# One-core decoder layer on Trainium2: spectral weights folded first and piece by piece, value projection moved into attention step 0, three later weights split during mixing steps 0 and 1

## The chip, the cores and the metric

The kernel runs on one core of a Trainium2 chip. The metric is the device time of one execution in microseconds (us). The engines are named as in the profile: PE is TensorE (its weight loads are PEld), DVE is VectorE, ACT is ScalarE, POOL is GpSimd, and SP is SyncE, which issues all DMAs of this kernel.

## The reference, cut to what matters

Eight sequences of 512 tokens of width 512 go through three sublayers, each with a residual and a layer norm:

```python
qkv = x @ w_qkv                        # 512 x 1536, then an FFT over each head of 64
kv = cumsum(fft(k) * fft(v), axis=1)   # along the tokens
x = layernorm(x + ifft(kv * conj(fft(q))).real @ w_out)

q, k, v = x @ W_q + b_q, ctx @ W_k + b_k, ctx @ W_v + b_v    # ctx: 8 x 77 rows, 16 heads of 32
x = layernorm(x + softmax(mask(q @ k.T / sqrt(32))) @ v @ W_o + b_o)

w = clip(round(kernel / s), -8, 7) * s           # s = max|kernel| / 7
x = layernorm(x + x @ w + bias + (x @ a) @ b)
```

## The kernel before, in words

The program has three stages, each a block with its own instruction list for every engine. The order in every list is written by hand; semaphores tie the lists together.

**Preparation (`prepare`).** It turns inputs and weights into what the loops need. Every operand of a big product is held as a high part of reduced precision (fp32r, written by ACT) and a low remainder (a subtraction by DVE or POOL), and each product is three matmuls: high by high, low by high, high by low (`split_matmuls`, line 74). In order: the 616 context rows are transposed and split; keys are projected (8 products of 12 matmuls of 308 columns) and stored to `k_dram`; values are projected (5 products of 12 matmuls of 512 columns) and stored to `v_dram`; then `w_qkv` is folded with the forward transform in 12 pieces (`turn`, then 4 products with `fwd`, which the profile counts as 8 matmuls of 128 columns) into `w_spec`; DVE quantizes the feed-forward weight in three passes of 128 x 2048 and adds the low-rank product `a @ b` (4 matmuls, `AT_LOW`); `w_out` is folded with the inverse transform (4 pieces, `AT_BACK`) into `w_back`. `raw_v` and `w_qkv` share the tile `wqkv_sb`, so most of `w_qkv` is loaded only after the split of `W_v`.

**Mixing (`mix_tokens`).** One step for each sequence. A step of PE is twelve spectral projections of 12 matmuls of 512 columns (v, v, k, k, q, q, twice), the four transposes (`turn`) of the next sequence's `x` between the first of them, and the four back projections of the sequence before. All four transposes use one PSUM bank, `xT_ps`: `turn(c)` waits until ACT and DVE have split piece c-1 (`split_x`, counted by `x_hi` and `x_lo`). Sequence 0 is transposed and split at the head of this stage. After step 0 ACT and POOL split `W_q`.

**Attention (`attend`).** Step i scores sequence i, and finishes sequence i-1. Step 0 has no earlier sequence: PE scores, transposes the probabilities, transposes `x1` of sequence 1 and projects its queries. Four PSUM banks are handed round in the order `START_ORDER`. `W_o` and the feed-forward weight are loaded raw at the head of the stage and split at the end of step 0 (by ACT and DVE, and by ACT and POOL).

Of the kernel before, what the change touches and what calls it, by code (L numbers as in the profile page):

```python
# [6 lines left out]
F32 = mybir.dt.float32  # L19
# [6 lines left out]
P = 128  # L26
# [51 lines left out]
def prepare(nc, ins, constants, half_power, ident, w_spec, w_back, k_dram, v_dram, ffn_dram, x_first, x_loaded, ffn,  # L78
            out_slots, w_k, w_v):


# [6 lines left out]
    with ExitStack() as ctx:  # L88
# [4 lines left out]
        fwd = sb("fwd_sb", [P, P])  # L93
        wT = sb("wT_sb", [P, 2, NC, P])


        ctx_tail = ffn[:, 0, :]
        inv = wqkv_sb[:, 0, 0:512].rearrange("p (h n) -> p h n", h=2)
        b_sb = wqkv_sb[0:RANK, 0, D:2 * D]

        raw_k = wout_sb[:]
        raw_v = wqkv_sb[:].rearrange("p c n -> p (c n)")[:, NC * D:2 * NC * D].rearrange("p (c n) -> p c n", c=NC)
        ctxT = [sb(f"ctxT_{k}", [P, NC, rows], F32R) for k in ("hi", "lo")]
        a_sb = ffn[:, 1, 0:NC * RANK].rearrange("p (c n) -> p c n", c=NC)
        aT = sb("aT", [RANK, D])
        bias_k = sb("bias_k", [P, NC])
        k_val = wT[:].rearrange("p a c n -> p (a c n)")[:, 0:2 * half_rows].rearrange("p (a n) -> p a n", a=2)

        out_hi, out_lo = out_slots
        SLOTS = NC  # L110
        top, top_all = sb("top", [P, 1]), sb("top_all", [P, 1])
        scale, per_scale = sb("q_scale", [P, 1]), sb("q_per_scale", [P, 1])
        turned = [ps(f"turned{n}", [P, NC * P]) for n in range(2)]
        prod = [ps(f"prod{n}", [P, D]) for n in range(2)]
        ident_loaded, constants_loaded = sem("ident_loaded"), sem("constants_loaded")
        ctx_loaded, wk_loaded, wv_loaded = sem("ctx_loaded"), sem("wk_loaded"), sem("wv_loaded")
        kernel_loaded, a_loaded, b_loaded = sem("kernel_loaded"), sem("a_loaded"), sem("b_loaded")
        fwd_loaded, qkv_loaded, out_loaded = sem("fwd_loaded"), [sem(f"qkv_loaded{r}") for r in range(NC)], sem("out_loaded")
        ctx_turned, tail_turned, ctx_hi, ctx_lo = sem("ctx_turned"), sem("tail_turned"), sem("ctx_hi"), sem("ctx_lo")
        a_turned, aT_ready, w_turned, wT_ready = sem("a_turned"), sem("aT_ready"), sem("w_turned"), sem("wT_ready")  # L120
        wk_hi_ready, wk_lo_ready, wv_hi_ready, wv_lo_ready = sem("wk_hi_ready"), sem("wk_lo_ready"), sem("wv_hi_ready"), sem("wv_lo_ready")
        prod_ready, prod_used = sem("prod_ready"), sem("prod_used")
        k_biased, k_hi_ready, k_lo_ready = sem("k_biased"), sem("k_hi_ready"), sem("k_lo_ready")
        v_hi_ready, fold_hi_ready = sem("v_hi_ready"), sem("fold_hi_ready")
        stored = [sem(f"kv_stored{n}") for n in range(SLOTS)]
# [6 lines left out]
        NKEY, NVAL = 2 * NC, len(tiles)  # L132
        GROUP = [(r, s) for r in range(NC) for s in range(3)]
        AT_V = NKEY
        AT_FOLD = AT_V + NVAL
        AT_LOW = AT_FOLD + len(GROUP)
        AT_BACK = AT_LOW + NC

        def fold_target(n):

            if n < len(GROUP):
                r, s = GROUP[n]
                return [w[:, r, s, :] for w in w_spec]
            return [w[:, n - len(GROUP), :] for w in w_back]

        def fold_place(n):
            return AT_FOLD + n if n < len(GROUP) else AT_BACK + n - len(GROUP)

        @block.sync
        def _(sp):  # L150
            flat = ins["ctx"].rearrange("b k d -> (b k) d")
            sp.dma_start(ident[:], ins["identity"]).then_inc(ident_loaded, 16)
            sp.dma_start(x_first[:], flat[0:tail, :].rearrange("(n p) d -> p n d", p=P)).then_inc(ctx_loaded, 16)
# [8 lines left out]
            for n in range(NKEY):  # L162
# [11 lines left out]
                elif 1 <= n < NC:  # L174

                    sp.wait_ge(wv_lo_ready, NC)
                    sp.dma_start(wqkv_sb[:, n, :], ins["w_qkv"][n * P:(n + 1) * P, :]).then_inc(qkv_loaded[n], 16)
# [1816 lines left out]
```

## Time and profile before

| | us |
|---|---|
| median of 3 runs | 968.82 |
| lowest and highest run | 965.21, 971.74 |
| span of the profiled execution, first to last instruction | 964.6 |
| PE busy in that span | 917.6 |
| DVE, ACT, POOL busy | 666.7, 376.8, 337.8 |

The times are of the whole execution; the span leaves out what lies before the first and behind the last instruction. The profiled execution has no time of its own in the list; its span is 0.6 us under the lowest run and 4.2 us under the median. Busy time of PE counts matmuls from their start to a modelled end, so a busy PE can still run at half clock.

### The profile page before, as it was taken

The page shows a single profiled execution, that of the slowest core. Times are in us where ns is not written, and L with a number is a line of the kernel's source. Part 1 is how long each engine was busy: PE and PEld are TensorE (multiplying, and loading weights), DVE is VectorE, ACT ScalarE, POOL GpSimd, SP SyncE. Part 2 cuts the span into 40 slices and gives each one's busy share as a digit, 9 for nine tenths or more (in the row PEclk, how much of TensorE's full clock was granted, in tenths as well). Part 3 has the DMA queues.
Part 4 walks back from the last instruction along what each step waited for, and adds up shares of the span by engine and source line. Part 5 has one row for each costly group of instructions (what it writes and reads, how often), then busy time and mean ns, then how long its engine had stood idle before and what let it go on. Part 6 is the DMA issues. An engine that isn't in the chain of part 4 may idle for free.

```text
span 964.6 us, 14638 instructions
## 1 busy us (share of the span) xinstructions
PE 917.6 (95%) x4476; PEld 754.5 (78%) x4476; DVE 666.7 (69%) x1128; ACT 376.8 (39%) x1403; POOL 337.8 (35%) x310
## 2 busy tenths in 40 slices
PE   5898999999999999999779999999999999999987
PEld 4784888888888888888668788888888888888775
DVE  3363466665656565555667888979889798887957
ACT  3152120101010111102287566656567565666610
POOL 2000243232222232324236434444443444433733
PEclk9998999999999999999979999999999999999999
DMA  5944201221203020203423122131222203120021
GB/s 179 326 148 172 90 1 52 80 80 52 104 28 127 3 87 1 88 23 116 134 81 102 25 79 73 40 113 24 89 63 78 75 21 122 30 89 21 17 77 44
DMA packets 72346, 76.02 MB, mean 79 GB/s; under 512 B 38567, under 2 KB 40871, under 8 KB 72303
## 3 DMA queue, kind: packets, MB, share of 16 engines
q1 hardware_dynamic: 72303, 75.49, 24.4%
q8 instruction: 22, 0.36, 0.2%
q14 instruction: 21, 0.17, 0.1%
HBM read 52.60 MB, written 22.87 MB: 78 GB/s over the span
## 4 chain that ended last, share of the span: by engine, by line
PE 41%; DVE 4%; ACT 2%; issue 2%; POOL 2%; POOLq 0%; DVEq 0%
PE shared_ps L74 31%; PE score_ps L74 4%; PE shared_ps L1146 4%; ACT probs L1352 2%; PE shared_ps L1109 1%; PE shared_ps L1179 1%; POOL probs L1501 1%; DVE score_ps L1658 1%; DVE xT_lo L1615 0%; DVE x_and_res L1704 0%; DVE top_s L1663 0%; DVE pT_lo L1642 0%; POOL x_and_res L1516 0%; DVE y L1682 0%; DVE w_o_lo L1825 0%
## 5 line engine op out<-in xcount | busy, mean ns | idle before, releaser
L1352 ACT ACTIVATE probs<-score_ps,top_s 128x77 f32<-128x77 f32 x512 | 159.0, 359 | 36.9 <-DVE top_s L1663 36.9
L1352 ACT ACTIVATION_READ_ACCUMULATOR probs<-score_ps,top_s 128x1 f32 x512 | 122.9, 240 | 0.0
L1501 POOL TENSOR_TENSOR probs<-probs,per_total 128x616 f32<-128x616 f32 x64 | 82.7, 1309 | 65.9 <-DVE per_total L1670 65.7
L1494 POOL TENSOR_TENSOR rstd<-ve,half_power 128x1 f32<-128x1 f32 x64 | 42.4, 662 | 157.1 <-DVE ve L1693 152.5
L722 POOL TENSOR_TENSOR vals<-qs_prod 128x512 f32<-128x512 f32 x32 | 41.1, 1296 | 127.1 <-DVE qs_prod L804 127.1
L713 POOL TENSOR_TENSOR mix_rstd<-mix_ve,half_power 128x1 f32<-128x1 f32 x32 | 22.0, 688 | 175.4 <-DVE mix_ve L823 175.4
L1658 DVE COPY_PREDICATED score_ps<-hidden,masked 128x616 f32<-128x616 int32 x64 | 66.2, 1034 | 11.6 <-PE score_ps L74 11.6
L1359 ACT ACTIVATE pT_hi<-shared_ps 103x512 fp32r<-103x512 f32 (+1 forms) x96 | 54.7, 612 | 46.0 <-PE shared_ps L1146 45.5
L672 ACT ACTIVATE v_sb<-v_ps 128x512 f32<-128x512 f32 x32 | 18.9, 594 | 133.9 <-PE v_ps L74 133.9
L679 ACT ACTIVATE qT_hi<-vals 128x512 fp32r<-128x512 f32 x32 | 19.4, 631 | 122.3 <-POOL vals L722 106.2
L1642 DVE TENSOR_TENSOR pT_lo<-shared_ps,pT_hi 103x512 fp32r<-103x512 f32 (+1 forms) x96 | 64.5, 684 | 0.0
L1146 PE MATMUL shared_ps<-ident,probs 128*103 128x128 f32 (+1 forms) x384 | 53.9, 279 | 2.6 <-POOL probs L1501 1.8
L74 PE MATMUL shared_ps<-w_o_hi,xT_hi 128*128 128x512 f32 x128 | 53.3, 417 | 2.3 <-DVE xT_lo L1623 1.9
L74 PE MATMUL shared_ps<-w_ffn_hi,xT_hi 128*128 128x512 f32 x120 | 50.1, 418 | 5.5 <-DVE xT_lo L1615 4.9
L1516 POOL TENSOR_TENSOR x_and_res<-x_and_res,bias_f 128x512 f32<-128x512 f32 x32 | 42.2, 1318 | 35.9 <-DVE x_and_res L1704 23.1
L1146 PEld LDWEIGHTS shared_ps<-ident,probs 128*103 128x103 f32 (+1 forms) x384 | 47.0, 158 | 9.7 <-POOL probs L1501 2.7
L1663 DVE TENSOR_REDUCE top_s<-score_ps 128x8 f32<-128x616 f32 x64 | 51.2, 800 | 3.6
L815 DVE TENSOR_TENSOR mix_r<-out_ps,x_res 128x512 f32<-128x512 f32 x29 | 20.1, 692 | 47.3 <-PE out_ps L74 47.3
L74 PE MATMUL v_ps<-xT_hi,w_spec_hi 128*128 128x512 f32 x128 | 50.6, 395 | 1.9 <-DVE xT_lo L766 1.9
L74 PE MATMUL k_ps<-xT_hi,w_spec_hi 128*128 128x512 f32 x128 | 51.7, 404 | 0.0
L74 PE MATMUL q_ps<-xT_hi,w_spec_hi 128*128 128x512 f32 x128 | 51.2, 400 | 0.0
L74 PE MATMUL shared_ps<-w_o_hi,xT_lo 128*128 128x512 f32 x128 | 50.7, 396 | 0.0
(218 smaller groups left out, 2660.1 us busy)
## 6 DMA issues: line engine op xcount, KB each, us to landing
x_tok<-in_x SPq DMA_DIRECT2D x8, 1024.0 KB, 5.9
x_res<-in_x SPq DMA_DIRECT2D x8, 1024.0 KB, 8.0
x_between<-mix_x SPq DMA_DIRECT2D x32, 256.0 KB, 2.0
x<-x_between SPq DMA_DIRECT2D x8, 1024.0 KB, 5.5
x_tok<-x_between SPq DMA_DIRECT2D x8, 1024.0 KB, 5.7
out<-y_out SPq DMA_DIRECT2D x32, 256.0 KB, 2.0
wqkv_sb<-in_w_qkv SPq DMA_DIRECT2D x4, 768.0 KB, 7.8
keys_split<-w_q_hi SPq DMA_DIRECT2D x8, 154.0 KB, 5.4
```

The costliest lines, as they stand in the source:

```text
L74: last = nc.tensor.matmul(out, l, r, start=(n == 0), stop=(n == len(terms) - 1))
L713: nc.gpsimd.tensor_tensor(rstd[:, t % 2:t % 2 + 1], ve[:, t % 2:t % 2 + 1], half_power[:], ALU.pow).then_inc(rstd_ready, 1)
L722: nc.gpsimd.tensor_tensor(vals[:, h, :], qs[:, 2 * h, :], qs[:, 2 * h + 1, :], ALU.subtract if h else ALU.add).then_inc(vals_summed, 1)
L1146: last = nc.tensor.transpose(shared_ps[s.bank(use)][0:size, g * P:(g + 1) * P], probs[:, t % 2, g * GK + at:g * GK + at + size], ident[:])
L1352: nc.scalar.activation(probs[:, t % 2, j * KEYS:(j + 1) * KEYS], score_ps[:, g, k * KEYS:(k + 1) * KEYS], ACT.Exp, bias=top[:, t % 2, j:j ...
L1359: nc.scalar.activation(pT[0][0:size, c, :, t * P:(t + 1) * P], turned_bank(s, t, c), ACT.Copy).then_inc(turned_hi, 1)
L1494: nc.gpsimd.tensor_tensor(rstd[:, n:n + 1], ve[:, n:n + 1], half_power[:], ALU.pow).then_inc(rstd_ready, 1)
L1501: nc.gpsimd.tensor_tensor(p, p, per_total[:, t % 2, h * heads:(h + 1) * heads].unsqueeze(2) .to_broadcast([P, heads, KEYS]), ALU.mult).the ...
L1516: nc.gpsimd.tensor_tensor(res2[:, t % 2, :], x2[:, t % 2, :], bias_f[:], ALU.add).then_inc(res2_ready, 1)
L1642: nc.vector.tensor_tensor(pT[1][0:size, c, :, tok], turned_bank(s, t, c), pT[0][0:size, c, :, tok].bitcast(F32), ALU.subtract).then_inc(fr ...
L1658: nc.vector.copy_predicated(s4, hidden[:, t, :].unsqueeze(1).unsqueeze(1).to_broadcast(shape), masked[:].unsqueeze(1).unsqueeze(1).to_broa ...
L1663: nc.vector.tensor_reduce(top[:, t % 2, h * 8:(h + 1) * 8].rearrange("p (g j) -> p g j", j=GH), s4, AX.X, ALU.max, negate=True).then_inc(t ...
```

## The change

- **Preparation** loads `w_qkv` first, in 12 pieces of 256 KB with a semaphore each, and folds them as they land. From the seventh piece on the transposes of the context ride along in four new PSUM banks (`side`, `turn_side`). Then come sequence 0 of `x`, the key projection, the low-rank product and `w_back`. The value projection is gone; the turned context is stored to a new DRAM tensor `c_dram` instead. Sequence 0 of `x` leaves this stage transposed and split. The quantization moves from DVE to POOL.
- **Mixing** starts with the projections at once. In steps 0 and 1 ACT and POOL also split `W_v`, `W_o` and the feed-forward weight, a quarter at a time through two pairs of slots, and SP stores both parts to `w_later` in DRAM. Each of the three is loaded into `x1_next` once the one before is done.
- **Attention** step 0 gets the value projection (`project_v`, 5 products of 12 matmuls, with `split_v` on ACT and DVE); split weights and turned context come from DRAM.

The core of the diff:

```diff
@@ prepare, sync @@
+            load_qkv(0, 0)
+            sp.dma_start(fwd[:], ins["dft_forward"]).then_inc(fwd_loaded, 16)
+            load_qkv(0, 1)
+            load_qkv(0, 2)
...
+            for r in (2, 3):
+                for s in range(3):
+                    load_qkv(r, s)
+            sp.dma_start(raw_k[:], by_chunk(ins["W_k"])).then_inc(wk_loaded, 16)
...
+                if n < len(tiles):
+                    at, size = tiles[n]
+                    for part, tile in enumerate(ctxT):
+                        sp.dma_start(c_dram[n, part, :, :, 0:size], tile[:, :, at:at + size].bitcast(F32)).then_inc(ctx_stored, 16)
@@ prepare, gpsimd @@
+            nc.gpsimd.tensor_scalar(ffn, ffn, per_scale[:], ROUND_MAGIC, ALU.mult, ALU.add).then_inc(quantized, 1)
...
+            nc.gpsimd.tensor_scalar(ffn, ffn, ROUND_MAGIC, -QMAX - 1, ALU.subtract, ALU.max).then_inc(quantized, 1)
...
+            nc.gpsimd.tensor_scalar(ffn, ffn, QMAX, scale[:], ALU.min, ALU.mult).then_inc(quantized, 1)
@@ mix_tokens, sync @@
-            load_x(2, 0, True)
+            load_x(2, 0, False)
+            load_residual(0)
+            for w, raw in enumerate(raw_later):
+
+                if w == 0:
+                    sp.wait_ge(wq_lo, NC)
+                else:
+                    sp.wait_ge(later_lo, w * NC)
+                sp.dma_start(x1_next[:], raw.rearrange("(c p) n -> p c n", p=P)).then_inc(later_loaded, 16)
+                for c in range(NC):
+                    n = w * NC + c
+                    sp.wait_ge(later_hi, n + 1)
+                    sp.wait_ge(later_lo, n + 1)
+                    for part in range(2):
+                        sp.dma_start(w_later[w, part, c * P:(c + 1) * P, :],
+                                     slots[n % 2][part].bitcast(F32)).then_inc(later_stored[n % 2], 16)
@@ mix_tokens, scalar @@
+            def split_later(w):
+
+                act.wait_ge(later_loaded, 16 * (w + 1))
+                for c in range(NC):
+                    n = w * NC + c
+                    wait_reuse(act, later_stored[n % 2], 32 * (n // 2))
+                    nc.scalar.activation(slots[n % 2][0], x1_next[:, c, :], ACT.Copy).then_inc(later_hi, 1)
...
+            split_later(0)
+            copy_v(0, 1, 0)
+            copy_v(0, 1, 1)
+            split_vals(0, 0, 0)
+            split_vals(0, 0, 1)
+            split_later(1)
+            split_vals(0, 1, 0)
+            split_vals(0, 1, 1)
+
+            copy_v(1, 0, 0)
+            copy_v(1, 0, 1)
+            split_later(2)
+            for c in range(NC):
+                split_x(2, 0, c)
@@ attend, sync @@
+            sp.dma_start(w_v[0].bitcast(F32), by_chunk(w_later[0, 0])).then_inc(w_v_loaded, 16)
+            load_context(0)
+            sp.dma_start(w_v[1].bitcast(F32), by_chunk(w_later[0, 1])).then_inc(w_v_loaded, 16)
@@ attend, tensor @@
             score(0, s, 1, 0)
+            project_v(s, 0)
             score(0, s, 1, 1)
+            project_v(s, 1)
             score(0, s, 2, 0)
             turn_probs(0, s, 0, 0)
             turn_probs(0, s, 0, 1)
             turn_probs(0, s, 0, 2)
+            project_v(s, 2)
...
+            project_v(s, 3)
             turn_probs(0, s, 1, 2)
             score(0, s, 3, 1)
             project_q(1, s, 0)
+            project_v(s, 4)
@@ attend, scalar @@
-            act.wait_ge(w_loaded[0], 16)
-            nc.scalar.activation(w_o[0][:], raw_o, ACT.Copy).then_inc(w_hi, 1)
...
-            act.wait_ge(w_loaded[1], 16)
-            nc.scalar.activation(w_ffn[0][:], raw_ffn, ACT.Copy).then_inc(w_hi, 1)
```

On POOL, `split_later(w)` (the remainders, counted by `later_lo`) stands in step 0 behind the `W_q` remainders for w = 0, behind the first two `remainder` calls for w = 1, and at the head of step 1 for w = 2.

## Rows read from the trace of the kernel before

**Rows 1.** The page: busy tenths of PE in 40 slices of 24.1 us.

```profile
PE   5898999999999999999779999999999999999987
```

**Rows 2.** Stretches by stage: preparation, mixing step 1, attention start.

```profile
0.00:88.00 88.00, 70.31 (x364) 55.01 (x364) 37.27 (x60) 31.81 (x59) 5.68 (x10) 0.94 0.58 192
...
125.70:165.00 39.30, 39.30 (x178) 31.59 (x178) 21.66 (x36) 8.69 (x13) 16.40 (x15) 1.00 0.05 19
...
475.00:500.00 25.00, 16.46 (x70) 15.05 (x71) 14.66 (x23) 17.84 (x102) 8.25 (x6) 0.66 0.46 146
```

The columns are start and end, length, busy time (with instructions) of PE, PEld, DVE, ACT and POOL, granted clock, DMA share, GB/s.

**Rows 3.** Timeline of PE: preparation and first mixing product (start, length).

```profile
17.20 0.59 PE L74 MATMUL prod<-ctxT_hi,xT_hi 128*128 128x308 f32 x1 [2.42 <-DVE xT_lo L352]
...
21.70 0.31 PE L74 MATMUL prod<-ctxT_lo,xT_hi 128*128 128x308 f32 x1
...
32.95 0.39 PE L74 MATMUL prod<-xT_hi,ctxT_hi 128*128 128x512 f32 x1
...
53.80 0.60 PE L251 MATMUL turned<-ident,wqkv_sb 128*128 128x128 f32 x4
54.24 1.06 PE L266 MATMUL prod<-fwd_sb,wT_sb 128*128 128x128 f32 x8
55.13 0.60 PE L251 MATMUL turned<-ident,wqkv_sb 128*128 128x128 f32 x4
...
71.26 4.03 PE L275 MATMUL prod<-wqkv_sb,aT 16*128 16x512 f32 x6 [0.36 <-DVE w_spec_lo L393]
75.22 9.36 PE L282 MATMUL prod<-wout_sb,wqkv_sb 128*128 128x512 f32 x16
...
90.09 0.51 PE L74 MATMUL v_ps<-xT_hi,w_spec_hi 128*128 128x512 f32 x1 [1.90 <-DVE xT_lo L766]
```

**Rows 4.** Two stretches of the first loads, with columns as in Rows 2.

```profile
3.00:4.00 1.00, 0.00 (x0) 0.00 (x0) 0.00 (x0) 0.00 (x0) 0.00 (x0) 1.00 0.77 219
4.00:5.00 1.00, 0.00 (x0) 0.00 (x0) 0.00 (x0) 0.00 (x0) 0.00 (x0) 1.00 1.07 387
```

**Rows 5.** Timeline of DVE in the preparation.

```profile
50.11 2.28 DVE L382 TENSOR_REDUCE top<-x 128x1 f32<-128x2048 f32 x1
...
71.12 0.68 DVE L411 TENSOR_TENSOR x<-prod,x 128x512 f32<-128x512 f32 x1
```

**Rows 6.** Groups of POOL by line: busy us, mean ns of one.

```profile
L335 POOL TENSOR_TENSOR xT_lo<-wqkv_sb,xT_hi 128x512 fp32r<-128x512 f32 x4 | 5.0, 1279 | 17.6 <-ACT xT_hi L299 17.6
...
L758 POOL MEMSET xT_hi<- 128x1232 f32 x1 | 1.1, 1130 | 0.0
```

**Rows 7.** DMA issues with us to landing: mixing start, one store, attention start.

```profile
x_tok<-in_x SPq DMA_DIRECT2D x1, 1024.0 KB, 5.1
...
x<-in_W_q SPq DMA_DIRECT2D x1, 1024.0 KB, 8.0
...
x_between<-mix_x SPq DMA_DIRECT2D x1, 256.0 KB, 2.0
...
x_tok<-in_W_o SPq DMA_DIRECT2D x1, 1024.0 KB, 6.7
```

**Rows 8.** Timeline of SP: the first DMAs of mixing and of attention.

```profile
86.22 0.38 SPq L515 DMA_DIRECT2D x_tok<-in_x  x1
...
475.46 0.39 SPq L1033 DMA_DIRECT2D x<-x_between  x1
```

**Rows 9.** Timeline of PE: two transposes in mixing step 1.

```profile
131.13 0.60 PE L565 MATMUL xT_ps<-ident,x_tok 128*128 128x128 f32 x4
134.43 0.66 PE L565 MATMUL xT_ps<-ident,x_tok 128*128 128x128 f32 x4
```

**Rows 10.** Timeline of PE in attention step 0, and the start of step 1.

```profile
484.29 0.62 PE L74 MATMUL score_ps<-xT_hi,qT_hi 128*128 128x308 f32 x1 [1.08 <-ACT probs L1352]
...
503.42 0.40 PE L74 MATMUL shared_ps<-xT_hi,w_q_hi 128*128 128x512 f32 x1
...
517.91 0.30 PE L74 MATMUL score_ps<-xT_hi,qT_hi 128*128 128x308 f32 x1
```

More of the change, by code:

```diff
@@ new lines, in _ @@
+            pe.wait_ge(ident_loaded, 16)
+            turn(0)
+            pe.wait_ge(fwd_loaded, 16)
+            for m in range(NFOLD):
+                if m + 1 < NFOLD:
+                    turn(m + 1)
+                if m == FIRST_SIDE:
+                    pe.wait_ge(ctx_loaded, 32)
+                if m >= FIRST_SIDE:
+                    turn_side(m - FIRST_SIDE)
+                pe.wait_ge(wT_ready, m + 1)
+                wait_reuse(pe, prod_used, m - 1)
+                for c in range(NC):
+                    p, h = c // 2, c % 2
+                    out = prod[m % 2][:, p * 256:(p + 1) * 256].rearrange("q (i h k) -> q i h k", i=2, h=2)[:, :, h, :]
+                    last = nc.tensor.matmul(out, wT[:, m % 2, c, :], fwd[:].rearrange("q (i k) -> q i k", i=2),
+                                            start=True, stop=True)
+                last.then_inc(prod_ready, 1)
@@ L620, in step @@
                     project(i, half, s, 1, h)
-            for c in range(NC):
-                turn(0, 0, c, first_banks[c])
             step(0, 0, True, False)
+            step(1, 1, True, True)
             steps(pe, step)
@@ L691, in step @@
                         split_vals(i, p, h)
+            copy_v(0, 0, 0)
+            copy_v(0, 0, 1)
+            split_x(1, 1, 0)
+            act.wait_ge(wq_loaded, 16)
             for c in range(NC):
[L694 to L697 removed]
+                nc.scalar.activation(w_q[0][:, c, :], x1_next[:, c, :], ACT.Copy).then_inc(wq_hi, 1)
+            split_x(1, 1, 1)
+            split_x(1, 1, 2)
+            split_x(1, 1, 3)
+            split_later(0)
[9 more added lines that the diff above has]
+            split_later(2)
+            for c in range(NC):
+                split_x(2, 0, c)
+            copy_v(1, 1, 0)
+            copy_v(1, 1, 1)
+            for p in range(PAIRS):
+                for h in range(2):
+                    split_vals(1, p, h)
             steps(act, step)
@@ L861, in step @@
                 times_q(i, 1, 1)
-            for c in range(NC):
-                split_x(0, 0, c, first_banks[c])
             step(0, 0, True, False)
+            step(1, 1, True, True)
             steps(dve, step)
@@ L916, in __init__ @@
         count = lambda kinds: sum(u[0] in kinds for u in BANK_ORDER)
+        values = sum(u[0] == "W" for u in START_ORDER)
+        first = isinstance(i, int) and i == 0
+        if first:
+            values = 0
+        self.turn = 0 if first else len(START_ORDER) % RING
         if isinstance(i, int):
             nexts, fronts, backs = min(i + 1, B), min(max(i, 0), B), max(i - 1, 0)
-            self.before = count(NEXT) * nexts + count(FRONT) * fronts + count(BACK) * backs
+            self.before = count(NEXT) * nexts + count(FRONT) * fronts + count(BACK) * backs + values
             self.filled_before = self.before - count(FRONT) * fronts
```

570 lines of the change are left out of this document (319 added, 251 removed).

## Prediction

> **What bounds the kernel now.** I read the page first, for where PE is not full: the slices are at 9 nearly everywhere but in the first four and in slices 20 and 21 [rows 1]. A table of stretches then cuts the time by stage. PE is busy 70.3 of the first 88 us, and every microsecond of mixing step 1 (39.3 of 39.3, clock 1.00), while at the start of attention it is busy 16.5 of 25 us at a clock of 0.66 [rows 2]. So three readings decide. The preparation is a serial piece of 90.09 us before the first mixing product [rows 3]; what is cut from it is won. A mixing step has no room on PE, so any new wait of PE there is lost in full. The head of attention has idle PE time that can hide added products. Behind these readings lie the timelines of PE, DVE and SP, the groups of POOL, and the landing times of DMAs.
>
> **Preparation: when does mixing start?** Built up from zero.
> *First fold.* Pieces of 256 KB follow the identity on the queue. The rate is 219 GB/s in the fourth microsecond and 387 GB/s in the fifth [rows 4], so the first piece's bytes are through at about 4.3 us. A 1 MB load alone lands in 5.1 us [rows 7], of which 1.05 MB at 387 GB/s is 2.7; of the fixed 2.4 I put half behind the bytes. The first transposes start at about 5.5. Later pieces come every 0.26 MB / 387 GB/s = 0.7 us, faster than they are folded, so DMA binds only once.
> *Fold.* From transposes to transposes one piece takes 55.13 - 53.80 = 1.33 us at full clock, of it 0.44 the transposes [rows 3]. Twelve are 16.0; six side transposes are 6 x 0.44 = 2.7. PE starts at half clock: the key products run at a pitch of 0.26 us from 17.20 until 21.70, and at 0.142 behind it (79 in 11.25 us) [rows 3]. So about 4.4 us run at half speed, 2.2 extra. Head and tail of the pipe 1.5, ACT and DVE copies of the side pieces on the fold's chain 1. The fold ends at 5.5 + 16.0 + 2.7 + 2.2 + 1.5 + 1 = 28.9.
> *Keys.* They need the remainders of W_k, four on DVE at about 0.68 [rows 5], behind the first high part and the last fold's split: 4 us. They start at 33, with 0.8 for a dip of the clock behind that idle time. 96 x 0.142 = 13.7 follow; a DVE reduction of 2.28 [rows 5], now between the first keys, holds PE up by 0.6. DVE is done at about 49.9.
> *Quantization on POOL.* DVE first does four splits of x (2.7), the reduction and three key tiles, so the scale is ready 9.3 us behind the start of keys, at 43.1. No row shows a scalar operation on POOL. A fill takes 1130 ns for 1232 columns (0.92 ns each), a subtraction of two tensors 1279 ns for 512 (2.5 ns each) [rows 6]. Three passes of 2048 columns lie between 5.6 and 15.4 us. One operand is read and two operations are made, so I take 3.0 each, nearer to the fill: ready at 52.1, 2.2 behind DVE. Bounds: 49.9 (DVE) and 58.5.
> *Rest.* From the first low-rank addition (71.12 [rows 5]) to mixing's first DMA (86.22 [rows 8]) it is 15.1 us. Two of the four low-rank products are now done ahead, 1 less. Much of this ran at half clock, so 2.5 less is the bound below. Mixing starts at 52.1 + 14.1 = 66.2 (61.5 to 72.6). Its first product needs nothing more, as x is already split. Against 90.09 that is **-23.9 us** (-28.6 to -17.5). The stores of turned context (2.6 MB) and of keys (2.5 MB) end before that at 387 GB/s, and at half of it.
>
> One rule speaks against the quantization's move. The Trainium skill, "GPSIMD Engine Reference", section 3.1, puts GpSimd at about 2.6 cycles an element where VectorE needs about 1. By that figure (an estimate, at the 1.2 GHz it names) three passes take 13.3 us instead of my 9.0, and mixing starts 4.3 us later. The trace agrees for two operands (2.5 ns each [rows 6]); the page itself puts that figure down to two inputs sharing a read port.
>
> **Mixing steps 0 and 1: the new chain.** From mixing's start (0 here). The loads of x and W_q are issued as before: W_q lands at 0.4 + 8.0 = 8.4 [rows 7]. ACT's first quarter 0.6, POOL's four remainders 5.0 [rows 6]: 14.1. SP then issues W_v, alone on the queue, 5.1 to land [rows 7]: 19.4.
> One weight through the slots, from its landing t: high part 0 to t+0.6, remainder to t+1.9; SP issues two stores, the second 0.4 behind the first, and a store lands in 2.0 [rows 7], slightly more as a pair: slot free at t+4.9, the other one remainder (1.28) later at t+6.1. The last high part ends at t+6.7, the last remainder at t+8.1. SP issues the last pair and the next load (0.9) which lands behind 0.5 MB of stores (5.1 + 0.7): t+14.9. So the second weight lands at 34.4, the third at 49.3, and its last high part ends at 56.0. In between ACT must do copy_v, and POOL two sums and two remainders of about 1.3; they fit.
> ACT has split_x(2,0,c) *behind* split_later(2), and the transposes share one bank. So turn(1) of step 1 waits until 56.0 + 0.6 (ACT) + 0.7 (DVE) = 57.3. PE reaches it much sooner. Step 0 takes as before 131.13 - 90.09 - 5.6 = 35.4, since two projections (2 x 2.8) stand ahead of turn(0) [rows 3, 9]; then two projections, one transposition and one projection, that is 5.6 + 134.43 - 131.13 = 8.9 [rows 9]: 44.3. PE stands still for 13 us. Nothing hides it: the row of step 1 shows no idle PE [rows 2]. Behind an idle stretch the clock is at half for about 4.4 us (as above), 2.2 more. **+15.2 us.** Bounds: landings and stores 0.5 us faster or slower six times, and no clock dip: 10 to 18.
> What else queues there: SP's store(0) and load of x(3) wait behind the weights, but are wanted only in step 2; POOL's sums of step 0 end some 4 us before PE wants them. The old W_q split cost PE nothing, so its move gains nothing.
>
> **Attention step 0.** Five products of 12 matmuls at 2.8 us are 14.0 of PE. It lasts now from 475.5 to 517.9 [rows 8, 10]. The first needs both parts of W_v and a context tile, 2.6 MB: 2.4 + 6.8 = 9.2 behind the start, 484.8. Even now the fourth score product waits 1.08 us for ACT's exponentials, until 484.29 [rows 10]; the bank order makes the new products wait for them too. Walking the list with these waits: W0 485 to 489.7 (mostly half clock), W1 to 493.2, W2 496 to 498.8, W3 508.6 to 511.4, the first query projection 512.7 instead of 503.42 [rows 10], and W4 another 2.8. Step 1 starts at 530: **+12.1 us**. Bounds: 2, if the products only fill idle time (8.5 us of 25) and lift the clock from 0.66 [rows 2]; 14, if none does. I take the walk, since exponentials are pushed back by the products ahead of them. The two weight splits that go from its end had no PE wait of note. The loads of W_o and of the feed-forward weight (4.2 MB, 11 us) land before project_o wants them, 12 us into step 1; the residual comes at about 538, as late relative to the step as now. I cost these at nothing; without the cover it would be 1 to 3 us.
>
> **Sum.** -23.9 + 15.2 + 12.1 = +3.4 on the profiled execution. Its span, 964.6, lies 4.2 under the median of 968.8; a difference made on it carries over: 968.8 + 3.4 = **972 us**.
>
> **Rivals.**
> *No wait in mixing.* The weights pass through the slots before PE comes to turn(1). For it: spare DMA capacity (share 0.05 in step 1 [rows 2]). Against it: the chain is latency, three times 15 us. It would give 968.8 - 23.9 + 12.1 = 957. Chance 0.13.
> *The value projection is hidden.* For it: 8.5 us of idle PE and the clock of 0.66. Against it: W_v's landing and the bank order. With 2 instead of 12.1: 962. Chance 0.17.
> *Slower: POOL becomes the bound of the preparation.* At the two-operand rate the passes take 15.4, the low-rank additions start at 58.5 and mixing at 72.6. It costs from 2.3 us a pass on, three for every one. 972.2 + 6.4 = 979, with 14 for attention 981. Chance 0.2. By the skill's figure, above, it would be 977.
> *The fold isn't early.* If pieces land late or out of step with PE, up to 5 us of the gain go: 977. This is within the forecast's range.
>
> **Chances.** Forecast (966 to 978) 0.5; the three rivals 0.13, 0.17 and 0.2. The range runs from just under the first rival to the slower one, 955 to 982. A difference of 1%, 9.7 us, is about what a measurement of this kernel can tell from none. Faster than 959: 0.2 (the first rival, part of the second); slower than 978.5: 0.27 (most of the third, the forecast's upper edge); between 0.53.
>
> **What would show it.** Right: first mixing product near 66 us; POOL's passes near 3 us each; in mixing step 1 one PE wait of some 13 us at turn(1), released by the split of x, with ACT waiting for stores and for the load of the third weight; half clock behind it; attention step 0 about 12 us longer. Wrong: a full PE row in mixing step 1, a first mixing product beyond 72, or an attention step 0 of 45 us. What would break it most is a DMA pair that lands in well under 2 us or over 3, since six of them lie in series.

## The result, and the profile after

| us | before | after |
|---|---|---|
| median (4 runs each) | 967.13 | **989.66** |
| lowest, highest | 965.21, 971.74 | 988.01, 992.13 |
| span of the profiled execution | 964.6 | 987.1 |
| granted clock over the span | 0.982 | 0.969 |

The changed kernel is slower by 2.3%: ratio 1.0234, 95% interval 1.02 to 1.0268. The prediction was 972, range 955 to 982. The measured time is above the range. The forecast of the difference was +3.4 us; it is +22.5, on the medians and on the spans alike.

I read the page of the changed kernel first, as I did for before [rows 1].

```profile
PE   8849949999999999999679899999999999999997
...
PEclk9959979999999999999889999999999999999999
...
PE 39%; DVE 3%; DMA 2%; ACT 2%; POOL 2%; issue 2%; SPq 0%; DVEq 0%; POOLq 0%; ACTq 0%
```

A slice is 24.7 us. The 4 in the third slice (49 to 74 us) and the one in the sixth (123 to 148 us) are two holes of PE of some 15 us each. The start of attention still reads 6 and 7. The third row is the chain that ended last: PE has 39% of it, and DMA has 2%.

The difference is best cut at three instants that both timelines of PE show: the first product of mixing, the first score product of attention, and the first score product of its step 1.

| us | mixing starts at | mixing lasts | attention step 0 | rest | span |
|---|---|---|---|---|---|
| before | 90.1 | 385.5 | 42.3 | 446.7 | 964.6 |
| after | 77.9 | 401.9 | 60.8 | 446.6 | 987.1 |
| difference | -12.2 | +16.4 | +18.4 | -0.1 | +22.5 |
| predicted | -23.9 | +15.2 | +12.1 | 0 | +3.4 |

**Preparation.** The timeline of PE of the changed kernel, with columns as in [rows 3]:

```profile
4.35 1.08 PE L211 MATMUL turned<-ident,wqkv_sb 128*128 128x128 f32 x4 [4.35 <-DMA wqkv_sb<-in_w_qkv]
...
44.96 1.98 PE L275 MATMUL prod<-b_sb,aT 16*128 16x512 f32 x4
62.50 3.78 PE L275 MATMUL prod<-b_sb,aT 16*128 16x512 f32 x4 [15.56 <-DVEq L398]
66.21 10.02 PE L282 MATMUL prod<-wout_sb,inv_sb 128*128 128x512 f32 x16
77.91 0.47 PE L62 MATMUL v_ps<-xT_hi,w_spec_hi 128*128 128x512 f32 x1 [1.68 <-PEq L73]
```

The first piece is turned at 4.35. The key products start at 30.3 and end by 45. Behind them and two low-rank products made ahead PE stands still for 15.56 us. The timeline of POOL says why:

```profile
37.51 0.38 POOL L331 PARTITION_ALL_REDUCE top_all<-top  x1 [36.67 <-DVE top L385]
45.11 1.96 POOL L334 TENSOR_SCALAR wqkv_sb<-wqkv_sb,q_per_scale 128x2048 f32<-128x2048 f32 x1 [7.22 <-issue]
47.16 7.21 POOL L336 TENSOR_SCALAR wqkv_sb<-wqkv_sb 128x2048 f32<-128x2048 f32 x1
54.48 7.18 POOL L339 TENSOR_SCALAR wqkv_sb<-wqkv_sb,q_scale 128x2048 f32<-128x2048 f32 x1
```

DVE has `per_scale` ready at 40.0. The first pass starts 5.1 us later, and the second and third take 7.2 us each. The low-rank additions of DVE, and with them the banks that PE needs, wait for the end of the third, 61.66.

**Mixing.** First the turn that waits, on PE; then ACT: the four quarters of the third weight (L683; `w_stage` and `bias_o` are the two slots) and, behind them, the split of `x` that the turn waits for (L675); then two stretches of 10 us, with columns as in [rows 2].

```profile
137.19 1.12 PE L575 MATMUL xT_ps<-ident,x_tok 128*128 128x128 f32 x4 [14.90 <-DVE xT_lo L828]
```

```profile
129.18 0.63 ACT L683 ACTIVATE w_stage<-x 128x512 fp32r<-128x512 f32 x1 [3.12 <-DMA x<-ffn_weight]
...
134.00 0.63 ACT L683 ACTIVATE w_stage<-x 128x512 fp32r<-128x512 f32 x1 [3.67 <-DMA weights_split<-w_stage]
135.30 0.63 ACT L683 ACTIVATE bias_o<-x 128x512 fp32r<-128x512 f32 x1 [0.67 <-DMA weights_split<-bias_f]
135.83 0.58 ACT L675 ACTIVATE xT_hi<-xT_ps 128x512 fp32r<-128x512 f32 x1
```

```profile
120.00:130.00 10.00, 2.29 (x10) 1.50 (x8) 0.00 (x0) 3.65 (x7) 6.93 (x7) 0.83 0.65 210
130.00:140.00 10.00, 2.81 (x9) 2.42 (x10) 2.58 (x4) 2.67 (x5) 4.95 (x4) 0.50 0.62 215
```

The split of `x` comes directly behind the last quarter of the third weight. PE has waited for it since 122.3, and the granted clock falls to 0.50, the lower of its two levels. Step 1 of before had 39.3 busy of 39.3 us [rows 2].

**Attention step 0.** Timeline of PE, the places with waits:

```profile
485.55 1.91 PE L62 MATMUL score_ps<-xT_and_qT 128*128 128x308 f32 x6 [3.84 <-ACT probs L1481]
489.18 5.49 PE L62 MATMUL shared_ps<-w_o_and_ffn 128*128 128x512 f32 x12 [1.72 <-DMA w_o_and_ffn<-weights_split]
...
512.83 1.18 PE L1259 MATMUL shared_ps<-ident,probs 128*103 128x128 f32 x4 [2.46 <-DVE xT_lo L1748]
515.07 4.91 PE L62 MATMUL shared_ps<-w_o_and_ffn 128*128 128x512 f32 x12 [1.06 <-DVE xT_lo L1748]
519.82 0.60 PE L1259 MATMUL shared_ps<-ident,probs 128*102 128x128 f32 x4
...
529.84 0.50 PE L62 MATMUL shared_ps<-xT_hi,w_q_hi 128*128 128x512 f32 x1 [2.20 <-DVE xT_and_qT L1756]
```

Two of the five products, W0 at 489.18 and W3 at 515.07, take 5.5 and 4.9 us instead of 2.9: they fall behind idle time, at half clock (granted 0.50 from 489.2 to 494.5, 0.58 from 515 to 520). And ACT shows what W3 does to the others:

```profile
520.50 0.33 ACT L1481 ACTIVATE probs<-score_ps,top_s 128x77 f32<-128x77 f32 x1 [5.86 <-PE shared_ps L1259]
```

These are the exponentials of tile 3. Their scores were done at 508.4. They overwrite the buffer of tile 1, so they wait for the last transposes of tile 1, at 519.82, and these stand behind `project_v(3)`. ACT splits the first query projection only behind the last exponentials of tile 3, at 528.28, although the products were through by 524.0, and the wait of 2.20 us at 529.84 is for this split.

### The profile page after: what moved, and what is told of

Read it like the earlier page. It is cut to its first block, busy times and chain, and to the rows that moved or that the text cites. A ratio compares the mean times of both kernels' runs of the same rounds, so it can differ in the third digit from the quotient of the medians.

```text
span 987.1 us, 14703 instructions
## 1 busy us (share of the span) xinstructions
PE 914.6 (93%) x4476; PEld 751.5 (76%) x4476; DVE 663.6 (67%) x1119; ACT 378.1 (38%) x1413; POOL 356.9 (36%) x317
## 4 chain that ended last, share of the span: by engine, by line
PE 39%; DVE 3%; DMA 2%; ACT 2%; POOL 2%; issue 2%; SPq 0%; DVEq 0%; POOLq 0%; ACTq 0%
PE shared_ps L62 30%; PE score_ps L62 4%; PE shared_ps L1259 3%; ACT probs L1481 2%; POOL probs L1640 1%; PE shared_ps L1292 1%; DMA values_split<-x_tok 1%; PE shared_ps L1222 1%; DMA w_o_and_ffn<-weights_split 1%; DVE score_ps L1800 1%; DMA x_tok<-x_between 1%; POOL x_tok L1647 0%; DVE x_and_res L1846 0%; DVE xT_and_qT L1748 0%; DVE top_s L1805 0%
## 5 line engine op out<-in xcount | busy, mean ns | idle before, releaser
L62 PE MATMUL shared_ps<-w_o_and_ffn,xT_and_qT 128*128 128x512 f32 x384 | 96.7, 401 | 4.2 <-DVE xT_and_qT L1748 3.5
L1633 POOL TENSOR_TENSOR rstd<-ve,half_power 128x1 f32<-128x1 f32 x64 | 42.3, 661 | 152.9 <-DVE ve L1835 148.4
L62 PE MATMUL shared_ps<-w_o_and_ffn,xT_hi 128*128 128x512 f32 x256 | 88.2, 407 | 2.2 <-DVE xT_lo L1756 1.8
L62 PEld LDWEIGHTS shared_ps<-w_o_and_ffn,xT_and_qT 128*128 128x128 f32 x384 | 70.1, 188 | 21.3 <-DVE xT_and_qT L1748 4.1
L62 PE MATMUL out_ps<-w_back_hi,xT_and_qT 128*128 128x512 f32 x224 | 71.0, 398 | 0.0
L62 PE MATMUL score_ps<-xT_and_qT 128*128 128x308 f32 x384 | 65.2, 312 | 5.8 <-ACT probs L1481 3.8
L1800 DVE COPY_PREDICATED score_ps<-hidden,masked 128x616 f32<-128x616 int32 x64 | 63.8, 996 | 4.2 <-PE score_ps L62 4.0
L62 PEld LDWEIGHTS score_ps<-xT_and_qT 128*128 128x128 f32 x384 | 58.8, 192 | 9.2 <-ACT probs L1481 4.1
L696 ACT ACTIVATE xT_and_qT<-vals 128x512 fp32r<-128x512 f32 x32 | 19.5, 631 | 114.9 <-POOL vals L762 99.0
L62 PEld LDWEIGHTS shared_ps<-w_o_and_ffn,xT_hi 128*128 128x128 f32 x256 | 48.8, 191 | 14.4 <-issue 2.8
```

The costliest lines, as they stand in the source:

```text
L62: last = nc.tensor.matmul(out, l, r, start=(n == 0), stop=(n == len(terms) - 1))
L1633: nc.gpsimd.tensor_tensor(rstd[:, n:n + 1], ve[:, n:n + 1], half_power[:], ALU.pow).then_inc(rstd_ready, 1)
L1800: nc.vector.copy_predicated(s4, hidden[:, t, :].unsqueeze(1).unsqueeze(1).to_broadcast(shape), masked[:].unsqueeze(1).unsqueeze(1).to_broa ...
```

## Experiments

All variants start from the changed kernel. Times are medians of 4 runs, ratios are to runs of the kernel before on the same chip; beside them stands the stage of the table above that the edit is aimed at. The runs fell on more than one chip; the medians of the kernel before lie between 966.3 and 967.1 on all of them, so a gain of 1 us in this table is no finding. The stages that an edit isn't aimed at move too: in dve_passes mixing and step 0 are 1.2 us longer each, and the rest is 3.3 shorter. Three variants (pool_cheap_forms, pool_warm and thin_products) leave a part of the computation out, as said with each.

| variant | median | ratio to before (95%) | what moved, after -> variant |
|---|---|---|---|
| changed kernel | 989.66 | 1.0234 (1.02, 1.0268) | |
| dve_passes | 976.47 | 1.0105 (1.0076, 1.0135) | mixing starts 77.9 -> 65.5 |
| pool_cheap_forms | 979.14 | 1.0137 (1.011, 1.0165) | 77.9 -> 66.8 |
| pool_warm | 978.81 | 1.0145 (1.011, 1.0179) | 77.9 -> 67.6 |
| splits_x_first | 981.24 | 1.0158 (1.0128, 1.0189) | mixing lasts 401.9 -> 392.5 |
| weights_apart | 972.11 | 1.0063 (1.0039, 1.0087) | 401.9 -> 386.0 |
| order_late_half | 988.33 | 1.0239 (1.0211, 1.0268) | step 0 60.8 -> 57.3 |
| order_step0 | 986.22 | 1.0203 (1.0174, 1.0233) | 60.8 -> 55.2, rest 446.6 -> 449.9 |
| residual_early | 980.93 | 1.0147 (1.012, 1.0174) | 60.8 -> 55.3, rest 446.6 -> 443.8 |
| thin_products | 984.27 | 1.0187 (1.0167, 1.0207) | 60.8 -> 57.7 |
| **all_four** | **952.86** | **0.9857 (0.9835, 0.9879)** | all of them |

### Term 1: the quantization

**dve_passes.** The three passes leave POOL's list and go to DVE:

```diff
+                if n == 3:
+                    dve.wait_ge(per_scale_ready, 1)
+                    nc.vector.tensor_scalar(ffn, ffn, per_scale[:], ROUND_MAGIC, ALU.mult, ALU.add).then_inc(quantized, 1)
+                if n == 5:
...
+            dve.wait_ge(quantized, 2)
+            nc.vector.tensor_scalar(ffn, ffn, QMAX, scale[:], ALU.min, ALU.mult).then_inc(quantized, 1)
```

> The changed kernel with the three quantization passes back on DVE, behind key tiles 3 and 5 and behind the last one. In the changed kernel per_scale is ready at 40.0, yet POOL's third pass ends at 61.66, and PE stands still for 15.6 us. Theory A (the passes on POOL bound the preparation): on DVE a pass takes 1.25 us in the trace of before, so the first low-rank addition starts near 48.5 instead of 61.7, 13 us earlier; PE then has hardly any idle time, w_back runs at full clock, 4 us less. Mixing starts at 61, and the execution takes 17 us less, 973. Rival B (the passes hold up the keys on DVE, and the clock stays at half): only 8 to 10 us less, 980. Rival C (mixing's start is bound by the stores of keys and context): mixing starts no earlier than 72, 984.

Measured: 13.2 us less (989.66 - 976.47), between A and B; C falls. Timeline of DVE:

```profile
42.71 1.28 DVE L386 TENSOR_SCALAR wqkv_sb<-wqkv_sb,q_per_scale 128x2048 f32<-128x2048 f32 x1
...
49.51 1.28 DVE L391 TENSOR_SCALAR wqkv_sb<-wqkv_sb,q_scale 128x2048 f32<-128x2048 f32 x1
50.82 0.69 DVE L396 TENSOR_TENSOR wqkv_sb<-prod,wqkv_sb 128x512 f32<-128x512 f32 x1
```

The first addition is at 50.8 instead of 61.7, and mixing starts 12.4 us earlier. That is as much as this term fell short (11.7). Of the four microseconds that A expected from a full clock 1.5 came: `w_back` took 8.5 us instead of 10.0, with its first 2.7 us still at a granted clock of 0.50.

**pool_forms** (one run, 996.58). Seven more POOL instructions on scratch data behind the three passes. It leaves no part of the computation out.

> The changed kernel with seven more POOL instructions on scratch tiles behind its three passes, for the price of each form by itself; its total time says nothing. In the trace the first pass (mult, add) shows 1.96 us, the other two (subtract, max and min, mult) 7.2. Theory A (POOL takes 7.2 us for any such pass of 128 x 2048 with two operations, 3.5 ns an element, and the record of the first pass starts too late: it really began at 39.9): mult with add takes 7.2 as soon as it follows another instruction, 3.6 for 1024 columns. Rival B (max and min are the dear ones, and the first pass only started late): mult with add takes 2.0, subtract with max 7.2. Rival C (contention with DVE makes them long): all forms fall to about 2 where DVE is idle.

Timeline of POOL, the added instructions:

```profile
62.34 1.90 POOL L345 TENSOR_SCALAR ctx_sb<-ctx_sb 128x2048 f32<-128x2048 f32 x1
64.33 1.89 POOL L347 TENSOR_SCALAR ctx_sb<-ctx_sb 128x2048 f32<-128x2048 f32 x1
66.30 7.09 POOL L349 TENSOR_SCALAR ctx_sb<-ctx_sb 128x2048 f32<-128x2048 f32 x1
73.47 5.38 POOL L351 TENSOR_SCALAR ctx_sb<-ctx_sb 128x2048 f32<-128x2048 f32 x1
78.94 1.04 POOL L353 TENSOR_SCALAR ctx_sb<-ctx_sb 128x1024 f32<-128x1024 f32 x1
80.05 1.89 POOL L355 COPY ctx_sb<-wout_sb 128x2048 f32<-128x2048 f32 x1
82.02 2.34 POOL L357 TENSOR_TENSOR ctx_sb<-ctx_sb 128x1024 f32<-128x1024 f32 x1
```

In order: multiply and add (twice), subtract and max, multiply alone, multiply and add on half the columns, a copy, a subtraction of two tensors. The starts follow each other, so the lengths can be trusted. A falls: multiply and add is short wherever it stands (0.93 ns an element), and subtract and max is long (3.5 ns) while DVE is mostly idle, so C falls too. B's times hold. Its reason, that max and min are the dear ones, is too narrow: a single multiplication is dearer (2.6 ns) than a multiplication with an addition. What makes a form dear stays open.

**pool_cheap_forms.** Passes 2 and 3 on POOL as multiply and add; the rounding is then not undone, and nothing is clipped:

```diff
-            nc.gpsimd.tensor_scalar(ffn, ffn, ROUND_MAGIC, -QMAX - 1, ALU.subtract, ALU.max).then_inc(quantized, 1)
+            nc.gpsimd.tensor_scalar(ffn, ffn, 1.0, 0.0, ALU.mult, ALU.add).then_inc(quantized, 1)
...
-            nc.gpsimd.tensor_scalar(ffn, ffn, QMAX, scale[:], ALU.min, ALU.mult).then_inc(quantized, 1)
+            nc.gpsimd.tensor_scalar(ffn, ffn, scale[:], 0.0, ALU.mult, ALU.add).then_inc(quantized, 1)
```

> The changed kernel with the second and third pass on POOL made with mult and add, like the first (the rounding is not undone and nothing is clipped, so the feed-forward weight is not the reference's). pool_forms showed mult with add at 1.9 us for 128 x 2048, subtract with max at 7.1. Theory A (the form of the operations is the price of the move, with a delay of 5.1 us before the first pass): passes at 45.1, 47.1 and 49.1, the last ends at 51 instead of 61.7, mixing starts at 67.3, and the execution takes 10.6 us less: 979. Rival B (the passes are long because of something else here, as DVE's remainders beside them): they stay at 7 us, 989.

Measured 979.14. The passes take 1.96, 2.00 and 2.07 us, and the last ends at 51.0: A holds. So the form of two instructions costs 10.5 us of the execution, on the same engine and at the same place. With these forms POOL is only 2.7 us behind DVE (979.14 against 976.47).

**pool_warm.** The same, with the same part left out, and with one small instruction behind the reduction over the partitions:

```diff
+            nc.gpsimd.tensor_scalar(warm[:], top[:], 1.0, 0.0, ALU.mult, ALU.add)
             pool.wait_ge(per_scale_ready, 1)
```

> pool_cheap_forms with one more POOL instruction of 128 x 1 (mult, add) directly behind the reduction over the partitions, which ends at 37.9, two microseconds before per_scale is ready (40.0). Theory A (the 5.1 us between per_scale and the first pass are a cost of the first such instruction behind the reduction over the partitions): the small instruction pays it from 37.9 on, the first pass starts at 43.0, 2.1 us earlier, and the execution takes 2 us less than pool_cheap_forms. Rival B (the delay comes from the wait or from the scalar operand in SBUF): the first pass stays at 45.1.

```profile
37.72 0.38 POOL L332 PARTITION_ALL_REDUCE top_all<-top  x1 [36.87 <-DVE top L387]
45.62 0.18 POOL L334 TENSOR_SCALAR warm<-top 128x1 f32<-128x1 f32 x1 [7.53 <-issue]
45.80 1.96 POOL L336 TENSOR_SCALAR wqkv_sb<-wqkv_sb,q_per_scale 128x2048 f32<-128x2048 f32 x1
```

No gain (978.81 against 979.14, intervals overlap), and the first pass starts no earlier, as B had it. But the small instruction waits for neither `per_scale` nor a scalar in SBUF, and it itself starts only 7.5 us behind the end of the reduction; the first pass follows it at once. So the delay belongs to the first instruction behind the reduction, as A said, and not to B's causes. A had its length wrong: it is 7.2 us from the reduction's end, not 5.1 from `per_scale`, and an instruction behind the reduction can't hide it. Data can't be what is waited for: in the changed kernel DVE reads the reduction's result at 39.65. What POOL does in that time no trace shows.

### Term 2: the order of splits in mixing

**splits_x_first.** On ACT, the four splits of `x` ahead of the third weight:

```diff
+            for c in range(NC):
+                split_x(2, 0, c)
             split_later(2)
-            for c in range(NC):
-                split_x(2, 0, c)
             copy_v(1, 1, 0)
```

> The changed kernel with one change on ACT: in mixing step 1 the four split_x(2,0,c) stand ahead of split_later(2). Theory A (the stall of 14.9 us at turn(1) is only ACT's place in the list): it goes in full, with the half clock behind it, 17 us less: 973, and PE has no idle stretch above 1 us in step 1. Rival B (the wait goes elsewhere: POOL's roots for the norms of step 0 still stand behind its split_later(2), which ends near 137 us): PE waits up to 5 us at the third or fourth back projection of step 1, 978. Rival C (the chain of weights then bounds step 2 through the store of x1 and the load of x): nothing gained, 990.

```profile
125.94 1.11 PE L575 MATMUL xT_ps<-ident,x_tok 128*128 128x128 f32 x4 [4.76 <-DVE xT_lo L828]
```

8.4 us less: half of what A expected. The stall fell from 14.90 to 4.76, at the same turn. Neither rival named this place. Ahead of the first `split_x` ACT still has `split_vals(0,1,1)`, which waits until 123.07 for POOL's sums, and POOL has the second half of W_o ahead of them. The stall hid a second, shorter chain.

**weights_apart.** The quarters of W_o are spread as well; ACT's list (POOL's remainders likewise, with quarters 2 and 3 behind the remainders of step 0):

```diff
-            split_later(1)
-            split_vals(0, 1, 0)
-            split_vals(0, 1, 1)
+            split_later(1, (0, 1))
             copy_v(1, 0, 0)
+            split_vals(0, 1, 0)
             copy_v(1, 0, 1)
-            split_later(2)
-            for c in range(NC):
+            split_x(2, 0, 0)
+            split_vals(0, 1, 1)
+            split_later(1, (2, 3))
+            for c in (1, 2, 3):
                 split_x(2, 0, c)
+            split_later(2)
```

> The changed kernel with ACT's and POOL's lists of mixing steps 0 and 1 reordered once more: splits_x_first still had 4.76 us at turn(1), because split_x(2,0,0) also stood behind split_vals(0,1,1), which waits for POOL's sums behind the second half of split_later(1). Now only the first two quarters of W_o stand ahead of copy_v(1,0,0), the other two between split_x(2,0,0) and split_x(2,0,1), and split_later(2) behind split_x(2,0,3); on POOL the last two quarters of W_o stand behind the remainders of step 0. Theory A (the stall is the places in the lists, and the chain of three weights has room in the 78 us of two steps): no wait of PE above 1 us in mixing steps 0 and 1, and 6 to 7 us less than splits_x_first: 974 (16 less than the changed kernel). Rival B (the chain is too long for two steps, so that POOL's roots or the loads behind it stop PE later in step 1 or in step 2): 978 to 982.

The page, busy tenths of PE:

```profile
PE   8849999999999999999679899999999999999987
```

972.11, 17.5 us less than the changed kernel. The hole of the sixth slice is gone, no wait of PE above 0.43 us is left in mixing, and mixing lasts 386.0 us, against 385.5 before. The same 24 splits and 24 stores are made; they cost PE nothing once no split of `x` stands behind them. B falls: its stop of PE for POOL's roots is that wait of 0.43 us (in all_four 1.48).

### Term 3: attention step 0

**thin_products.** `project_v` sums only the first quarter of the width, 3 matmuls of 12, so three quarters of the product are left out:

```diff
-                pieces = [([c[:, a, k, 0:size] for a in range(2)], [w[:, k, :] for w in w_v]) for k in range(NC)]
+                pieces = [([c[:, a, k, 0:size] for a in range(2)], [w[:, k, :] for w in w_v]) for k in range(1)]
```

> The changed kernel with project_v cut to 3 of its 12 matmuls (only the first quarter of the context's width is summed, so the values are not those of the reference); all waits, splits, stores and loads are kept. Theory A (of the 18.4 us of step 0, what is PE time of the products is 5 x 2.8, of it 9/12 would go, the rest is waits of exponentials and banks): between 7 and 9 us less, 981 to 983. Rival B (products fill time in which PE would wait for exponentials anyway, the chain of exponentials sets the length): 3 us or less gone, 987. Rival C (all PE time, and the half clock with it): 12 us or more, 977.

The median falls by 5.4, between A and B; step 0 by 3.1, as B has it. At 0.23 us each the 45 matmuls that are gone are 10.4 us of PE work. PE is busy 8.3 us less in the step (38.6 against 46.9) and idle 5.2 us more (19.0 against 13.9). Its longest waits are now for ACT's exponentials (5.18 us) and for DVE (3.70, 2.67 and 2.46), which frees banks and writes remainders. So in good part the chain of these two engines sets the pace here, and not PE.

**order_step0.** On PE (the lists of ACT and DVE and the order of banks follow):

```diff
-            project_v(s, 0)
             score(0, s, 1, 1)
-            project_v(s, 1)
+            project_v(s, 0)
             score(0, s, 2, 0)
+            project_v(s, 1)
...
-            project_v(s, 3)
             turn_probs(0, s, 1, 2)
             score(0, s, 3, 1)
+            project_v(s, 3)
```

> The changed kernel with another order in attention step 0, on PE, ACT and DVE alike: score(1,1) ahead of project_v(0) and score(2,0) ahead of project_v(1); turn_probs(1,2) and score(3,1) ahead of project_v(3), with W3 and P12 exchanged in the order of the banks. The products are the same. Theory A (a part of the 18.4 us is exponentials pushed back by products ahead of their scores: ACT stands 5.86 us before exponentials(3,0), which wait for the transposes of tile 1 behind project_v(3)): step 0 takes 4 to 6 us less than 60.8, execution 984 to 986. Rival B (the 18.4 us are the PE time of the products and the half clock): at most 1 us less, 989.

Step 0 takes 5.6 us less, as A expected, with all products in place. The execution gains only 3.4, because 3.3 us return in step 1, where PE waits 4.06 us instead of 2.61:

```profile
554.55 0.68 PE L1259 MATMUL shared_ps<-ident,probs 128*103 128x128 f32 x4 [4.06 <-POOL probs L1640]
```

Of the 3.3 us the longer wait is 1.5. The rest fits the clock behind it: the granted clock is 0.50 from 556.5 to 558.5, while the changed kernel, behind its 2.61 us, keeps 1.00.

**order_late_half** makes only the second of these two exchanges.

> Half of order_step0: only turn_probs(1,2) and score(3,1) ahead of project_v(3) (W3 and P12 exchanged), with W0 and W1 left where they were. order_step0 made step 0 5.6 us shorter. Theory A (both places push exponentials back): this half gives 2 to 3 us of the step's length, ACT's wait of 5.86 us before exponentials(3,0) is gone, execution 987.5. Rival B (only the last place in the chain counts, since later slack takes up what the first half gave): all of it, 986.

Step 0 takes 3.5 us less and the execution 1.3 (988.33, not told apart from the changed kernel by this many runs); the wait for POOL is there as well, 4.00 us. ACT's wait of 5.86 us is gone, as A said. So both places count, with 3.5 and 2.1 us of the 5.6, and A's size for this half was somewhat low for the step.

**residual_early.** On top of order_step0, on SP:

```diff
+            store_values(4)
             for k in range(2):
                 sp.dma_start(w_o[k].bitcast(F32), by_chunk(w_later[1, k])).then_inc(w_o_loaded, 16)
-            for k in range(2):
-                sp.dma_start(w_ffn[k].bitcast(F32), by_chunk(w_later[2, k])).then_inc(w_ffn_loaded, 16)
-            store_values(4)
             for n in range(2):
                 sp.wait_ge(v_stored[n], 32 * len(range(n, len(tiles), 2)))
             load_residual(0, first, False)
+            for k in range(2):
+                sp.dma_start(w_ffn[k].bitcast(F32), by_chunk(w_later[2, k])).then_inc(w_ffn_loaded, 16)
```

> order_step0 with one more change on SP at the end of attention step 0: store_values(4) ahead of the loads of W_o, and the load of the residual ahead of the two loads of the feed-forward weight (4.2 MB stood before it). In order_step0 the residual is issued at 540.3, POOL adds its bias from 546.0 to 552.1, and PE waits 4.06 us for the normalized probabilities behind it, at half clock afterwards. Theory A (that wait is the queue): the residual is issued 10 us earlier, the wait goes, 4 to 6 us less than 986.2: 981. Rival B (PE then waits for W_ffn or for DVE at the same place; before had 2.33 us of such a wait): 1 to 2 us less, 985.

Timelines of SP and POOL:

```profile
529.97 0.37 SPq L1117 DMA_DIRECT2D x_tok<-x_between  x1
```

```profile
539.20 5.59 POOL L1647 TENSOR_TENSOR x_tok<-x_tok,bias_o 128x512 f32<-128x512 f32 x4 [12.89 <-DMA x_tok<-x_between]
546.19 2.39 POOL L1640 TENSOR_TENSOR probs<-probs,per_total 128x616 f32<-128x616 f32 x2 [1.41 <-DVE per_total L1812]
```

The residual is issued at 530.0 instead of 540.3, POOL is done with its bias before the probabilities are wanted, and PE's wait is gone: 980.93, 5.3 us less than order_step0. A holds. Note that the residual is in use only 9.2 us behind its issue (5.5 in the changed kernel); 2.1 MB of `W_o` are issued just ahead of it. That these are the reason is likely, and not tested.

**all_four**: dve_passes, weights_apart, order_step0 and residual_early together.

> The changed kernel with dve_passes, weights_apart, order_step0 and residual_early together. If the four causes add up: 989.7 - 13.2 - 16 - 3.4 - 5 = 952, 1.5% faster than the kernel before (967). Rival: the causes share their gain (weights that land later relative to mixing, DMA that collides with stores): 957 to 962. If the kernel were bound by something not touched here (clock, DMA), not under 965.

```profile
PE   8889999999999999999789999999999999999997
...
PEclk9979999999999999999889999999999999999999
...
PE 45%; ACT 2%; DVE 2%; POOL 2%; issue 1%; POOLq 0%; DVEq 0%
```

952.86, as the sum of the four had it: 1.4% faster than the kernel before and 3.7% faster than the changed one. Both holes are gone, and DMA has left the chain. The stages: mixing starts at 65.1 and lasts 387.1; step 0 takes 54.8; the rest 443.3. Taken singly the edits gave 13.2, 17.5 and 8.7 (order_step0 with residual_early), in sum 39.4; together they gave 36.8. The rival, a loss of 5 us or more by sharing, falls.

## Why the prediction was wrong, by its own steps

**First fold, fold, keys: right, and a little pessimistic.** First transposes 4.35 (predicted 5.5), keys from 30.3 (33), last key product done at 45.0. One reading needs a caution. That PE "starts at half clock" was read from the pitch of the products. The profile's granted clock reads 1.00 in that stretch of before (17 to 22 us), and in the changed kernel it reads 1.00 as well from 4 to 10 us, while a transposition piece takes 1.08 us instead of 0.60. The slow start is real; whether it is the clock, these rows don't show.

**Quantization on POOL: the step that failed most, 9.6 us.** It read: "One operand is read and two operations are made, so I take 3.0 each, nearer to the fill". It put the end of the passes at 52.1; they ended at 61.7, beyond even the bound of 58.5. The scale was ready 3.1 us earlier than laid out (40.0), the first pass came 5.1 us behind it, and the three passes took 16.6 us instead of 9.0. I had the fill and the subtraction of two tensors as the two nearest rows and took them for ends of a scale. They aren't: with one operand read, 128 x 2048 took from 1.9 to 7.2 us by the operations alone, and the dearest form (3.5 ns an element) lies above my upper end (2.5). The 5.1 us ahead of the first pass are a wait that no step of mine had. The low-rank additions thus became the rival "POOL becomes the bound", 3.2 us later than it said. By the Trainium skill, "GPSIMD Engine Reference", section 3.1 (2.6 cycles an element), mixing would have started at 70.5 (an estimate); that was nearer to the measured 77.9 than my figure, but by luck: the page gives the figure for two inputs, and for one input the trace shows 0.93 ns in one form and 3.5 in another, where 2.6 cycles at 1.2 GHz are 2.2 (an estimate). A candidate for the delay is in the same page, section 2.1: the first call into freshly loaded GpSimd code costs about 6 us without an instruction in the profile. The traces show 7.0 to 7.6 us at that place, in all ten profiles that have an instruction there; that it is code loading, no run here shows.

**Rest of the preparation: 2.1 us off.** From the last pass to mixing's first product it took 16.3 instead of 14.1. PE had stood still for 15.6 us, and the granted clock was 0.50 from there until about 72, over the two low-rank products and more than half of `w_back` (10.0 us against 9.4 [rows 3]). dve_passes took 14.7.

**Mixing: mechanism right, size near.** +16.4 against +15.2: one wait at turn(1) of step 1, released by the split of `x`, of 14.9 us (predicted 13), the clock at half behind it. The chain W_q, W_v, W_o, feed-forward came 2.0 us later than I had laid it out, mostly since the loads behind stores took 7.1 and 6.3 us from issue to first split (W_o 106.71 to 113.84, feed-forward 122.92 to 129.18), where I had 5.8. splits_x_first shows that the wait had a second cause behind the first: my walk had gone to the last link alone.

**Attention step 0: 6.3 us short.** W0 started 9.4 us into the step (predicted 9.5). From there the walk fell behind: 1.4 us at W2, 2.2 at W3, 4.2 at the first query projection, 6.3 at the end. Its largest failure is W3. I had it at full clock, 2.8 us, and in nobody's way. It took 4.75, and it pushed the exponentials of tile 3 back to 520.5 by way of the transposes of tile 1, in front of which it stands: a dependency through a buffer of ACT that I hadn't followed. order_late_half, which only moves W3 behind those transposes and a score product, takes 3.5 us of the step back, and order_step0 5.6, by order alone. Step 0 then costs 12.9 us more than before. That this is near the 12.1 of my walk is chance, as the walk was made for the other order. I had written that "exponentials are pushed back by the products ahead of them" and then walked only PE's list.

**Loads behind step 0, costed at nothing: right for the sum, wrong for the reason.** The rest is equal to before (446.6 against 446.7). But the residual was late, issued 3.5 us into step 1 (1.3 before), and PE waited 2.61 us for POOL behind it; residual_early has 2.8 us less in the rest than the changed kernel. That the sum came out is luck: PE's wait of 2.33 us for DVE later in step 1 of before has shrunk to 0.57 us.

**Range.** Its upper end took one failure at a time. The preparation, mixing and attention step 0 all came out dearer than forecast, at once: 11.7 + 1.2 + 6.3 = 19.2, and with -0.1 for the rest that is the whole distance between the predicted and the measured difference, 22.5 - 3.4 = 19.1.

## What to carry to other kernels

Work that is moved to fill an idle engine costs by its place in that engine's list: ask of each moved instruction which short, urgent instruction now stands behind it, and walk the lists of all engines through the buffers, not only the one that is the bound. The same splits cost 16.4 us of mixing or 0.5, by their order alone. Price an operation that the trace doesn't show by its exact form, and where it isn't to be had, let the range reach to the dearest row per element times more than one. When a stall is removed, look for the next wait at the same instruction before calling the gain.

## What the runs showed of the hardware

- POOL, `tensor_scalar` of 128 x 2048 in SBUF: multiply and add 1.9 to 2.1 us; subtract and max 7.1 to 7.2; min and multiply 7.2; multiply alone 5.4; a copy 1.9. DVE takes 1.2 to 1.3 for each of the three passes (dve_passes).
- The first POOL instruction behind `PARTITION_ALL_REDUCE` started 7.0 to 7.6 us behind its end, in ten profiles, even one of 128 x 1.
- While POOL's passes ran in the changed kernel, one subtraction of DVE with all operands in SBUF (128 x 308, otherwise 0.48 us) took 4.79 us. Additions of DVE that read one operand from PSUM took their usual 0.69 us beside POOL's subtract and max in pool_forms. The Trainium skill, "SBUF — State Buffer", section "Who interferes with whom", has a port pair that DVE and GpSimd lock against each other. The trace agrees in kind: DVE was held, but only until 52.1, while POOL's pass ran until 54.4. It cost nothing here.
- PE behind an idle stretch of 15 us ran at the lower clock: a transposition piece of 0.60 us took 1.12 (granted clock 0.50 from 137 to 139).
